# Other PSUM banks for the first steps of a sequence, and the gate rows evicted ahead of two query blocks, in a 16-sequence recurrent and attention kernel

## What is computed

```
xn = layernorm(x)
# mixer 0: gated linear recurrence over tokens, 16 heads of 16
state = state * exp(logsigmoid(xn Wgk1 Wgk2 + b)/16) + v k^T ;  out = state q
# ffn 0: 8 experts, 2 used for each token
logits = xn @ w_gate ; top-2 ; softmax over the two -> gates (T x 8)
h   = relu(xn @ Wd[e] + bd[e])            # 8 experts x 64 = 512 hidden
y   = 0.5 * sum_e gates[:, e] * (h[e] @ Wu[e] + bu[e])
x   = x + recurrence * silu(y)
# layer 1: windowed attention, gated by a ternary-weight ffn
```

## Time and profile before

| | |
|---|---|
| median of 3 runs | 3416.82 us (3414.13 to 3417.32) |
| profiled execution | 3419.85 us |
| its span, first to last instruction | 3418.1 us |
| mean granted TensorE clock | 0.997 of full |
| busy share of the span | PE 96%, DVE 78%, ACT 54%, POOL 37% |
| one sequence | some 209 us (16 of them, and some 56 us of preparation) |

### The profile page before, as it was taken

The page is one execution under the profiler, slowest core; times in us unless marked ns, Lnnn a source line. Parts: engine busy times, 40 slices in busy tenths (PEclk is TensorE's granted clock), DMA queues, the critical chain, the costliest instruction groups (busy, mean ns, idle before and its releaser), DMA issues.

```text
span 3418.1 us, 89893 instructions
## 1 busy us (share of the span) xinstructions
PE 3286.0 (96%) x35134; PEld 2274.5 (67%) x35134; DVE 2671.5 (78%) x6395; ACT 1834.8 (54%) x4088; POOL 1272.6 (37%) x1404
## 2 busy tenths in 40 slices
PE   5999999999999999999999999999999999999998
PEld 3676666766667666676766667666676666766666
DVE  6877878878788777887778777787877878878787
ACT  3364654646546465463655636456364654646546
POOL 4434244242443524425233342423434244242432
PEclk9999999999999999999999999999999999999999
DMA  4002010020100202011020110202002010020110
GB/s 116 22 22 61 23 53 19 25 58 24 52 23 25 54 24 61 15 38 40 24 64 11 54 29 21 63 12 65 18 24 60 24 52 21 22 58 24 52 23 26
DMA packets 110005, 128.56 MB, mean 38 GB/s; under 512 B 23457, under 2 KB 77329, under 8 KB 109585
## 3 DMA queue, kind: packets, MB, share of 16 engines
q1 hardware_dynamic: 104720, 121.13, 13.7%
q10 hardware_dynamic: 4864, 1.69, 0.2%
HBM read 74.01 MB, written 17.30 MB: 27 GB/s over the span
## 4 chain that ended last, share of the span: by engine, by line
PE 71%; DVE 12%; ACT 7%; DMA 4%; issue 3%; POOL 1%; SPq 0%; DVEq 0%; ACTq 0%; POOLq 0%
PE bank L1926 7%; PE bank L1549 5%; PE bank L1945 5%; PE bank L1828 5%; PE bank L1694 4%; PE bank L1863 4%; PE bank L1889 4%; PE bank L1586 3%; DMA g_wide<-gate_rows 3%; PE bank L1711 3%; PE bank L1766 3%; PE bank L1666 3%; PE bank L1651 3%; DVE am L1268 3%; PE bank L1845 2%
## 5 line engine op out<-in xcount | busy, mean ns | idle before, releaser
L901 POOL TENSOR_TENSOR qx<-qx 128x512 f32<-128x512 f32 x256 | 277.5, 1084 | 656.9 <-ACT qx L1139 655.1
L1403 DVE TENSOR_REDUCE row_max<-bank 128x4 f32<-128x384 f32 x512 | 270.8, 550 | 90.6 <-PE bank L1828 90.1
L1268 DVE TENSOR_TENSOR am<-bank,causal 128x512 f32<-128x512 f32 x512 | 327.9, 682 | 17.6 <-PE bank L1666 17.6
L1509 DVE TENSOR_TENSOR sq_lo<-qx,sq_hi 128x512 fp32r<-128x512 f32 x256 | 232.3, 907 | 125.3 <-ACT sq_hi L1127 124.1
L1945 PE MATMUL bank<-pj_t,sq_hi 128*128 128x256 f32 x1024 | 260.3, 288 | 6.2 <-DVE sq_lo L1509 5.5
L1023 ACT ACTIVATE tanh_g<-bank 128x256 f32<-128x256 f32 x128 | 49.2, 384 | 400.8 <-PE bank L1549 400.8
L1549 PE MATMUL bank<-w_vg,xt 128*128 128x512 f32 x512 | 252.3, 615 | 0.0
L1945 PE MATMUL bank<-pj_t,sq_lo 128*128 128x256 f32 x1024 | 251.0, 279 | 0.0
L1586 PE MATMUL bank<-xt,w_down 128*128 128x512 f32 x512 | 237.2, 596 | 0.0
L1139 ACT ACTIVATE qx<-bank,scale_fc 128x512 f32<-128x512 f32 x256 | 177.2, 692 | 98.5 <-PE bank L1931 96.6
L1412 DVE TENSOR_TENSOR am<-bank,row_max 128x384 f32<-128x384 f32 x384 | 212.9, 554 | 9.8
(11 more groups left out here) (278 smaller groups left out, 8523.1 us busy)
## 6 DMA issues: line engine op xcount, KB each, us to landing
g_wide<-gate_rows SPq DMA_DIRECT2D x64, 512.0 KB, 6.1
x<-in_L_attn_x SPq DMA_DIRECT2D x128, 128.0 KB, 2.3
qt<-in_L_attn_x SPq DMA_DIRECT2D x128, 128.0 KB, 2.5
out<-x SPq DMA_DIRECT2D x128, 128.0 KB, 1.7
k<-k SPq DMA_DIRECT2D x96, 128.0 KB, 2.4
xl<-xh SPq DMA_DIRECT2D x48, 128.0 KB, 2.4
xl<-xn SPq DMA_DIRECT2D x48, 128.0 KB, 2.3
xh<-xn SPq DMA_DIRECT2D x48, 128.0 KB, 2.3
```

The costliest lines, as they stand in the source:

```text
L901: nc.gpsimd.tensor_tensor(sq[:, n % 3, :], relu[:, n % 3, :], relu[:, n % 3, :], ALU.mult)\
L1268: nc.vector.tensor_tensor(am_tiles[:, :, j], bank[3 + j][:].rearrange("p (f e t) -> p f e t", f=2, e=2), causal[:].unsqueeze(1).unsqueeze( ...
L1403: nc.vector.tensor_reduce(row_max[:, j, :], bank[1 + j][:, 0:4 * KW].rearrange("p (h k) -> p h k", k=KW), AX.X, ALU.max, negate=(j == 0)). ...
L1509: nc.vector.tensor_tensor(sq_lo[:, n % 3, :], sq[:, n % 3, :], sq_hi[:, n % 3, :].bitcast(F32), ALU.subtract)\
```

## The change

Three tables and waits are edited. In `first_queries_keys` keys 6 go to bank 2 in place of bank 6. In `experts_down` the hidden blocks 0 to 3 go to banks 2, 3, 7 and 6 in place of 0, 1, 2 and 3. So banks 1 and 0, into which the gates are turned, hold nothing when TensorE comes there, and the wait for two Relu evictions ahead of the turns goes. Blocks 2 and 3 wait instead for the copies of keys 3 and 2, keys 6 and 7 for Relu evictions 1 and 3, `cumulate(0)` for 2 Relu evictions in place of 4, and `parity_scores(0)` for the fourth. On ScalarE the two copies of gate rows come ahead of those of queries 4 and 5. Nothing is computed otherwise than before.

```
--- before.py
+++ after.py
@@ -303,6 +303,8 @@
     pair_turn_banks = (2, 1, 3)
     turn_banks = {6: 7, 7: 0}
     gate_banks = (1, 0)
+    down_banks = (2, 3, 7, 6)
+    first_banks = {2: 6, 3: 7, 4: 4, 5: 5, 6: 2, 7: 7}
     output_banks = (1, 1, 1, 1, 1, 1, 1, 7)
     up_banks = (2, 2, 2, 2, 2, 2, 2, 5)
     qk_banks = (5, 1, 6, 0)
@@ -915,7 +917,7 @@
                     def first_queries_keys(n):
                         g, which, half = n // 4, n // 2 % 2, n % 2
                         act.wait_ge(s["qkp_ok"], at("qkp_ok", n - 1))
-                        nc.scalar.copy((kt if which else qt)[:, half, g * 512:(g + 1) * 512], bank[4 + n % 4][:])\
+                        nc.scalar.copy((kt if which else qt)[:, half, g * 512:(g + 1) * 512], bank[first_banks[n]][:])\
                           .then_inc(s["qk_ok"], 1)
 
                     for i in range(NC // 2):
@@ -938,16 +940,16 @@
                         act.wait_ge(s["hp_ok"], at("hp_ok", i + 1))
                         if i == 4:
                             act.wait_ge(s["gkl_ok"], at("gkl_ok", NC // 2))
-                        nc.scalar.activation(hidden_t[g][:, j, :], bank[5 if g else j][:], ACT.Relu, bias=b_down[:, j:j + 1])\
+                        nc.scalar.activation(hidden_t[g][:, j, :], bank[5 if g else down_banks[j]][:], ACT.Relu, bias=b_down[:, j:j + 1])\
                           .then_inc(s["hr_ok"], 1)
 
                     experts_relu(0)
                     experts_relu(1)
-                    first_queries_keys(4)
-                    first_queries_keys(5)
                     for b in range(NG):
                         act.wait_ge(s["gtp_ok"], at("gtp_ok", b + 1))
                         nc.scalar.copy(gate_rows[:, b * 512:(b + 1) * 512], bank[gate_banks[b]][32:64, :]).then_inc(s["gx_ok"], 1)
+                    first_queries_keys(4)
+                    first_queries_keys(5)
                     experts_relu(2)
                     nc.scalar.activation(warm[:], gdiff[:, 0:1], ACT.Exp)
                     experts_relu(3)
@@ -1564,26 +1566,20 @@
                             if copy:
                                 pe.wait_ge(s["hqk_ok"], at("hqk_ok"))
                         elif n >= 6:
-                            pe.wait_ge(s["qk_ok"], at("qk_ok", n - 5))
+                            pe.wait_ge(s["hr_ok"], at("hr_ok", 1 if n == 6 else 3))
                         w = w_k if which else w_q
                         for k in range(KD):
-                            mm = nc.tensor.matmul(bank[4 + n % 4][:], w[:, k, half * P:(half + 1) * P],
+                            mm = nc.tensor.matmul(bank[first_banks[n]][:], w[:, k, half * P:(half + 1) * P],
                                                   xt[:, k, g * 512:(g + 1) * 512], start=(k == 0), stop=(k == KD - 1))
                         mm.then_inc(s["qkp_ok"], 1)
 
                     def experts_down(i):
 
                         g, j = i // 4, i % 4
-                        if i == 0:
-                            pass
-                            if copy:
-                                pe.wait_ge(s["lg_ok"], at("lg_ok"))
-                        elif i == 1:
-                            pass
-                            if copy:
-                                pe.wait_ge(s["hqk_ok"], at("hqk_ok"))
+                        if i in (2, 3):
+                            pe.wait_ge(s["qk_ok"], at("qk_ok", 4 - i))
                         for k in range(KD):
-                            mm = nc.tensor.matmul(bank[5 if g else j][:], w_down[:, k, j * P:(j + 1) * P],
+                            mm = nc.tensor.matmul(bank[5 if g else down_banks[j]][:], w_down[:, k, j * P:(j + 1) * P],
                                                   xt[:, k, g * 512:(g + 1) * 512], start=(k == 0), stop=(k == KD - 1))
                         mm.then_inc(s["hp_ok"], 1)
 
@@ -1594,7 +1590,8 @@
                     first_queries_keys(4)
                     first_queries_keys(5)
                     pe.wait_ge(s["gates_ok"], at("gates_ok", 7))
-                    pe.wait_ge(s["hr_ok"], at("hr_ok", 2))
+                    if copy:
+                        pe.wait_ge(s["lg_ok"], at("lg_ok"))
                     for b in range(NG):
                         for j in range(4):
                             mm = nc.tensor.transpose(bank[gate_banks[b]][:, j * P:(j + 1) * P], gates[:, 4 * b + j, :], ident[:])
@@ -1609,7 +1606,7 @@
                             pe.wait_ge(s["gkd_ok"], at("gkd_ok", 32 * (c // 2)))
                         if c == 0:
                             pe.wait_ge(s["qk_ok"], at("qk_ok", 3))
-                            pe.wait_ge(s["hr_ok"], at("hr_ok", 4))
+                            pe.wait_ge(s["hr_ok"], at("hr_ok", 2))
                         else:
                             pe.wait_ge(s["am_ok"], at("am_ok", 4 * c - 2))
                         first, second = gk_first[:, c, :], gk_second[:, c, :]
@@ -1658,6 +1655,7 @@
                         pe.wait_ge(s["dst_ok"], at("dst_ok", c + 1))
                         if c == 0:
                             pe.wait_ge(s["qk_ok"], at("qk_ok", 5))
+                            pe.wait_ge(s["hr_ok"], at("hr_ok", 4))
                         elif c <= 4:
                             pe.wait_ge(s["hr_ok"], at("hr_ok", 4 + c))
                         for half in range(2):
```

## The result

| | before | changed |
|---|---|---|
| median | 3416.85 us (6 runs, 3413.83 to 3421.83) | 3431.18 us (6 runs, 3425.46 to 3433.57) |
| ratio | | 1.004, 95% interval 1.0028 to 1.0053 |
| profiled span | 3418.1 us | 3427.5 us |
| mean granted clock | 0.997 | 0.992 or 0.993 in each of the six runs |

The changed kernel is slower by 14.3 us, 0.4%. The forecast was 1.6 us less, within 3409 to 3420. It is the third rival that came true, TensorE's clock, to which I had given 0.06.

What follows compares the result with a forecast made beforehand. TensorE's work makes up most of the chain, but once a sequence the end hangs on the gate rows' DMA spread. 1.4 + 0.2 = 1.6 us less gave execution 3418.2, or 3415.2 as median, range 3409 to 3420.

Steps and rivals of the forecast that it cites:

- third rival: TensorE's hole ahead of L1694 grows to 2.3 us and its clock halves: 1.7 us a sequence, 3441 us, chance 0.06.
- Where the gain would go: Gate rows start 0.98 us sooner, but SP's write stays behind the `x` loads; 0.1 us each taken, 1.4 in 14 sequences.
- The 6.1 us of slack: SP's write waits for ScalarE 0.44 us in each of 14 sequences; 6.1 us is all that can be gained there.
- The first sequence's 0.2: In the first sequence, loads long issued, gate rows wait only for the turned bank: 0 to 0.3 us gained, 0.2 taken.
- Rivals 1 and 2: SP's write: 1, all the queue's slack comes through, 3410.4 us, chance 0.18; 2, the full 0.98 us, 3402.1, chance 0.08.
- The new waits at 0: The changed bank waits on TensorE and ScalarE each have their release well ahead, so they cost 0.
- Closing the first hole widens the second by as much: TensorE's 1.38 us hole ahead of the gate turns moves to the one ahead of L1694, with no gain by itself.

Runs made afterwards that it cites:

- The two runs with `x` later: Loads of `x` moved behind the moves of the decays in SP's queue: in the kernel before, 3410.2 us; in the changed kernel, 3395.9 us.
- banks only: The changed kernel's banks and waits, with ScalarE evicting queries 4 and 5 ahead of the gate rows as in the kernel before: 3435.3 us.

## Why the prediction was wrong

*Where the gain would go.* Right in its mechanism: the gate rows came about 1 us sooner against the second Relu, and SP's queue kept it. The 6.1 us of slack went at the issue, and nearly all of it came back at the landing. The term's size, 0.1 us each or 1.4, is not shown: the ways give 0.03 each, 0.5 in all. The first sequence's 0.2 was right: its gate rows start 3.31 us behind the first Relu, 3.48 before. The two runs with `x` later show that both the issue and the landing were the loads' doing, as the earlier trace rows had suggested. Rivals 1 and 2 fell.

*The new waits at 0.* Right, as far as the runs can tell: with the wait ahead of the turns put back, all the others new, the kernel runs as before (ratio 0.9997 to 1.0015).

*"Closing the first hole widens the second by as much."* Near in size: 20.7 + 13.7 = 34.4 before, and 35.2 after, where the forecast had some 33. Wrong as a cost. The forecast priced a hole by its length alone, so that moving one was free. This is the step that failed. What the runs showed in its place: 35 us of idleness in two pieces (the wait put back) give the time of before, 3418.0, and the same 35 us in one piece give 3431.2, some 13 us more, since the clock fell to half at 8 of the 15 merged holes.

*The clock as a rival.* The mechanism stood in the text with its place and its price. What failed was its chance, 0.06, and the reason given for it: 2.3 us is nearer to the 1.4 of the earlier trace rows than to the 4.25 of the earlier trace rows. Being nearer was no reason. Nothing in the trace said which lengths between 1.4 and 4.25 are harmless. If the turning point lay somewhere between the two, each place as likely, a hole of 2.3 would be past it with 0.9 / 2.85, one chance in three (my estimate). The price was 1.7 us in all 15 sequences, 25 us; measured, 1.56 in 8 of them, 12.5 us.

*What decides whether it falls.* Not only the hole's length. In the changed kernel it fell behind holes of 2.02 and 2.83 us and stayed behind one of 2.76, as its timeline shows (the last two of these rows are followed by the falls at 920.70 and 1340.60 above, the first by none):

```profile
710.72 1.56 PE L1692 MATMUL bank<-w_up,qx 128*128 128x256 f32 x6 [2.76 <-POOL qx L855]
...
919.92 1.31 PE L1692 MATMUL bank<-w_up,qx 128*128 128x256 f32 x4 [2.02 <-POOL qx L855]
...
1340.21 1.33 PE L1692 MATMUL bank<-w_up,qx 128*128 128x256 f32 x3 [2.83 <-POOL qx L855]
```

In the ten traces together TensorE had, behind the first sequence, 119 holes of 0.9 to 2.0 us, and the clock fell at none of them. It had 33 of 2.0 to 3.6 us, and the clock fell at 24. The longest without a fall was one of 2.87 (banks only). What tells the 24 from the 9 is left open.

## What to carry to other kernels

Before a hole of a nearly full TensorE is moved, see what it merges with: two holes of 1.4 and 1.0 us, 12 us apart, cost nothing here beyond their own length; merged into one of 1.6 to 2.8 us they cost 1.6 us more in 8 of 15 cases. The busy share can't show this; look at the granted clock of the stretch behind the hole. And an earlier producer gained next to nothing here as long as its transfer stood behind a megabyte of others in the same queue. With the loads moved behind it, the same earlier rows were worth 14 us; the transfer split so that the part that is waited for lands first brought 18 more.

## What the runs showed of the hardware

The granted clock fell to 0.50 for 3.4 us at 24 of the 33 holes of 2.0 to 3.6 us that TensorE had inside the sequences, and at none of 119 holes of 0.9 to 2.0 us. 23 of the falls began 0.1 to 1.4 us behind the end of the hole, with TensorE busy again, and one began 0.35 us ahead of it. At the longer holes of the preparation in the kernel before (4.54 us up to 28.11, 5.03 us up to 43.09) the clock fell inside the hole, at 26.95 and 40.60, each time for 6.8 us.

SP's queue waited 1.16 us for a write of 16 KB from SBUF to DRAM to land when the loads of `x` were out of its way, and 1.53 and 1.82 us on average (the kernel before, the changed one) when 1 MB of loads had been issued ahead of it.
